# Xattn + FFN kernel: the first two feed-forward norm rows turned by VectorE block transposes and DMA copies instead of by TensorE

## The reference

```
x = x + attention(layernorm(x), ctx, ctx, mask)   # 32 query heads, 8 key heads, width 128, rope, softmax, wo
x = x + ffn(layernorm(x))                         # one 1024 x 1024 layer, weights decoded from 4 bit planes
...
y_l = jnp.einsum('bsi,oi->bso', x, w_l)           # w_l from lut4 and the planes of qweight
y = jnp.where(mask[..., None], y_h, y_l) + bias   # mask: norm of a row of x over 64
```

## Time and profile before

| | us |
|---|---|
| Median of 3 runs | 2346.12 (2346.0 to 2348.01) |
| The profiled execution: its own time | 2348.9 |
| Its span | 2347.1 |
| PE busy | 2331.3 (99%) |
| DVE busy | 1692.3 (72%) |
| ACT busy | 1113.4 (47%) |
| POOL busy | 569.7 (24%) |
| L957, the feed-forward's matmuls, x768 | 174.5, 389 ns each |

### The profile page before, as it was taken

How to read it: one execution, slowest core, us unless ns; L and a number is a source line. 1 busy time by engine, 2 the same in 40 slices (tenths; PEclk the granted TensorE clock), 3 DMA queues, 4 the chain that set the end, 5 groups by cost and what they waited for, 6 DMA issues and landing times.

```text
span 2347.1 us, 35131 instructions
## 1 busy us (share of the span) xinstructions
PE 2331.3 (99%) x11878; PEld 1990.4 (85%) x11878; DVE 1692.3 (72%) x3808; ACT 1113.4 (47%) x2469; POOL 569.7 (24%) x674
## 2 busy tenths in 40 slices
PE   9999999999999999999999999999999999999999
PEld 8999998788888888888888888888888888888887
DVE  8887777577777777776777667776777677777763
ACT  5555544546464646464544444454444444444110
POOL 1000001222232223232322223232323232331320
PEclk9999999999999999999999999999999999999999
DMA  7466558543344433434357733333433333334442
GB/s 265 152 205 207 192 179 296 161 118 117 108 129 121 119 117 113 135 108 126 108 154 233 228 95 113 108 109 91 120 104 108 102 109 109 91 110 159 156 137 81
DMA packets 330098, 328.26 MB, mean 140 GB/s; under 512 B 32448, under 2 KB 266176, under 8 KB 329920
## 3 DMA queue, kind: packets, MB, share of 16 engines
q1 hardware_dynamic: 294496, 309.88, 42.7%
q10 hardware_dynamic: 35424, 16.14, 2.7%
HBM read 181.73 MB, written 71.30 MB: 108 GB/s over the span
## 4 chain that ended last, share of the span: by engine, by line
PE 92%; DMA 3%; DVE 2%; ACT 1%; SPq 1%; issue 1%; POOL 0%; ACTq 0%; DVEq 0%
PE bank L917 28%; PE bank L831 28%; PE bank L785 8%; PE bank L957 7%; PE bank L888 7%; PE bank L847 7%; PE bank L762 6%; DMA small_split<-probs 2%; SPq L616 1%; POOL probs L1943 0%; DVE residual L1806 0%; PE bank L743 0%; DMA ln_row<-in_L_xattn_wk 0%; PE bank L723 0%; PE bank L862 0%
## 5 line engine op out<-in xcount | busy, mean ns | idle before, releaser
L831 PE MATMUL bank<-acts_split,weights_split 128*128 128x512 f32 (+1 forms) x3168 | 744.5, 384 | 0.0
L917 PE MATMUL bank<-weights_split,small_split 128*128 128x512 f32 x3072 | 741.0, 390 | 1.4 <-DVE small_split L1790 1.3
L917 PEld LDWEIGHTS bank<-weights_split,small_split 128*128 128x128 f32 x3072 | 574.4, 188 | 121.1 <-DVE small_split L1790 2.7
L831 PEld LDWEIGHTS bank<-acts_split,weights_split 128*128 128x128 f32 x3168 | 576.4, 189 | 111.1
L1943 POOL TENSOR_SCALAR probs<-probs,row_numbers 128x256 f32<-128x256 f32 x512 | 359.0, 713 | 1195.0 <-DVE row_numbers L1776 1195.0
L1250 ACT ACTIVATE probs<-bank,row_numbers 128x256 f32<-128x256 f32 x512 | 237.4, 471 | 127.5 <-DVE row_numbers L1771 127.5
L1780 DVE STREAM_TRANSPOSE probs<-probs 128x512 f32<-128x512 f32 x250 | 177.7, 711 | 144.5 <-POOL probs L1943 144.5
L1935 POOL TENSOR_TENSOR rope_x<-rope_x,sin_t 128x512 f32<-128x512 f32 (+1 forms) x132 | 166.6, 1262 | 406.5 <-ACT rope_x L1223 406.5
L1765 DVE CUSTOM_DVE_ANT_0 bank<-bank,mask_tile 128x256 f32<-128x256 f32 x512 | 207.1, 446 | 63.6 <-PE bank L847 63.4
L1785 DVE TENSOR_TENSOR small_split<-small_split 128x512 fp32r<-128x512 f32 x250 | 178.9, 715 | 89.5 <-ACT small_split L1263 89.3
L847 PEld LDWEIGHTS bank<-small_split 128*128 128x128 f32 x1536 | 217.8, 190 | 21.9 <-DVE small_split L1745 1.7
(11 more groups left out here) (124 smaller groups left out, 2167.5 us busy)
## 6 DMA issues: line engine op xcount, KB each, us to landing
small_split<-probs SPq DMA_DIRECT2D x754, 64.0 KB, 2.2
raw<-in_L_xattn_wq SPq DMA_DIRECT2D x61, 512.0 KB, 3.8
raw<-in_L_xattn_wo SPq DMA_DIRECT2D x60, 512.0 KB, 3.8
k_scratch<-small_split SPq DMA_DIRECT2D x64, 256.0 KB, 2.3
v_scratch<-small_split SPq DMA_DIRECT2D x32, 512.0 KB, 2.9
x_scratch<-raw SPq DMA_DIRECT2D x64, 256.0 KB, 2.8
acts_split<-x_scratch SPq DMA_DIRECT2D x32, 512.0 KB, 5.1
mask_tile<-in_mask_BxSxS_ff SPq DMA_DIRECT2D x64, 256.0 KB, 2.9
```

What stands on the lines that cost most here:

```text
L831: last = pe.matmul(query_bank(j)[:, 0:wide], wq_s[:, h, c, a, :], xT[:, c, m, b * S:b * S + wide], start=c == 0 and i == 0, stop=c == C - ...
L917: last = pe.matmul(out_ps[part][:, :], o_s[:, a, u % 2 * S + t * P:u % 2 * S + (t + 1) * P], wo_s[:, h, m, n * BANK:(n + 1) * BANK], start ...
```

## The change

`PE_ROWS` and `turn_rows` are gone: tiles 0 and 1 take the way of the others. Their steps are put at these places:

- Tile 0: `row_write` one unit earlier (unit NU-4) on VectorE, the block transpose in unit NU-3 where the write stood, the copies on SyncE ahead of weight load 0, `row_high` on ScalarE ahead of the last `turned_high`.
- Tile 1: `row_write` in unit NU-1, the block transpose ahead of `row_low(0)`, the copies on SyncE between the bias load and weight load 6, `row_high` ahead of the square roots of tiles 2 and 3, and `row_low(1)` ahead of `row_stats(2)` instead of behind the write and the transpose of tile 2.
- Tile 2: statistics, write and transpose stand behind `row_low(1)`; the factor of tile 3 is computed behind the transpose of tile 2 and no longer ahead of its write. The factors of tiles 0 and 1 stay where they were.

```diff
@@ SyncE: the copies around the weight loads
+            move_rows(0)
             for c in range(C):
                 if c == 0:
                     sp.wait_ge(rope_mm, B_ROPES)
                 elif c == REP:
                     sp.wait_ge(pT_tr, len(PE_TURNS))
                 elif c == REP + 2:
+                    move_rows(1)
                     sp.wait_ge(wide_mm, B_WIDE - BURST + 1)
...
-            def move_rows(f):
-
-                sp.wait_ge(ln_blocks, f - PE_ROWS + 1)
-                if f > PE_ROWS:
-                    sp.wait_ge(ln_lo, f)
...
-            move_rows(PE_ROWS)
+            move_rows(2)
@@ TensorE
             turn(NU - 1)
-            turn_rows(0)
             project(NU - 2, range(BURST // 2))
...
-                    if (n, c) == (NN - 1, C // 2 - 1) and f + 1 < PE_ROWS:
-                        turn_rows(f + 1)
@@ ScalarE
+                if f == 0:
+                    act.wait_ge(rope_mm, B_ROPES)
+                elif f >= HT:
+                    act.wait_ge(wide_mm, B_WIDE + (f - HT + 1) * NN)
+                act.wait_ge(rows_in, 4 * 16 * (f + 1))
...
             output_one_high(NU - 2)
+            row_high(0)
             turned_high(NU - 1)
-            row_high(0)
             output_one_high(NU - 1)
...
+            row_high(1)
@@ VectorE
                 if u == NU - 3:
-                    row_write(0)
+                    turn_row_blocks(0)
...
                 if u == NU - 1:
                     add_mask(u)
+                    row_write(1)
                 invert(u)
...
+                if u == NU - 4:
+                    row_write(0)
...
             output_one_low(NU - 2)
+            turn_row_blocks(1)
+            row_low(0)
             turned_low(NU - 1)
-            row_low(0)
             output_one_low(NU - 1)
-            row_write(1)
             add_projection(NU // REP - 1)
...
-            row_stats(PE_ROWS)
-            row_stats(PE_ROWS + 1)
-            row_factor(PE_ROWS)
-            row_factor(PE_ROWS + 1)
-            row_write(PE_ROWS)
-            turn_row_blocks(PE_ROWS)
             row_low(1)
+            row_stats(2)
+            row_stats(3)
+            rows(2)
+            turn_row_blocks(2)
+            row_factor(3)
```

More of the change, by code:

```diff
@@ L670, in _, with move_rows @@
                         load_rows(1, b)
+            def move_rows(f):
+                sp.wait_ge(ln_blocks, f + 1)
+                if f:
+                    sp.wait_ge(ln_lo, f)
+                for a in range(P // QUAD):
+                    sp.dma_start(rows_moved[:, a, :], ln_row[a * QUAD:(a + 1) * QUAD, :]).then_inc(rows_in, 16)
+            move_rows(0)
             for c in range(C):
@@ L726, in turn_row @@
                         last.then_inc(x_tr, 1)
[L728 to L736, removed]
             def turn_weights(tile):
@@ L1042, in row_high @@
                 t = f % HT
[L1043 to L1052, removed]
+                if f == 0:
[3 more added lines that the diff above has]
+                act.wait_ge(rows_in, 4 * 16 * (f + 1))
+                act.activation(xT[:, :, HI, t * P:(t + 1) * P].rearrange("p c (a q) -> p c a q", q=QUAD),
+                               row_blocks(), ACT.Copy).then_inc(ln_hi, 1)
             def piece_hi(k):
@@ L1338, in _ @@
             output_one_high(NU - 2)
+            row_high(0)
             turned_high(NU - 1)
-            row_high(0)
             output_one_high(NU - 1)
-            row_std(PE_ROWS)
-            row_std(PE_ROWS + 1)
+            row_high(1)
+            row_std(2)
+            row_std(3)
             for f in range(NT):
-                if f + 1 < NT:
+                if f and f + 1 < NT:
                     row_high(f + 1)
@@ L1448, in row_write @@
                 ln_steps.wait()
[L1449 to L1452, removed]
+                if f:
+                    dve.wait_ge(rows_in, 4 * 16 * f)
                 else:
                     dve.wait_ge(x_tr, 2 * NT)
[L1455 to L1459, removed]
-                                  acc[:, f % HT, :].rearrange("p (i m) -> p m i", i=QUAD))
+                row, total = (ln_row[:, :].rearrange("p (m i) -> p m i", i=QUAD),
+                              acc[:, f % HT, :].rearrange("p (i m) -> p m i", i=QUAD))
                 dve.tensor_scalar(row, total, ln_mv[:, s, 0:1],
@@ L1474, in row_low @@
                 dve.wait_ge(ln_hi, f + 1)
[L1475 to L1484 removed]
+                part = xT[:, :, :, f % HT * P:(f % HT + 1) * P].rearrange("p c l (a q) -> p l c a q", q=QUAD)
+                dve.tensor_tensor(part[:, LO], row_blocks(), part[:, HI].bitcast(F32),
+                                  ALU.subtract).then_inc(ln_lo, 1)
             def piece_lo(k):
```

22 lines of the change are left out of this document (4 added, 18 removed).

## The result

The changed kernel took 2351.75 us (median of 13 runs, 2348.67 to 2354.91), the kernel before 2347.39 us (13 runs, 2343.97 to 2353.32). The ratio is 1.0022, with a 95% interval from 1.0014 to 1.0029: 3.3 to 6.8 us more, where 2.7 were forecast. The profiled execution took 2353.45 us, with a span of 2351.6.

The account below looks back on a forecast made before the run. TensorE, busy 99% of the span, was taken to bound the kernel. Transposes -0.63 and -0.79, load 7 +0.8, the stand ahead of tile 2 +3.3: +2.7 us, from 2346.12 to 2348.8; range 2344.6 to 2352.8.

Parts of the forecast that it names:

- The cover: Ahead of tile 2: its split rows are ready at 2189.17, its start is 2191.32; the change draws on these 2.15 us.
- First transposes: TensorE ahead of the weighted values: removing the first eight transposes (0.79 us) starts tile 0 0.63 us earlier.
- Second: TensorE, the second removed group of eight transposes: 0.79 us saved, all on the path.
- Load 7: Tile 0, ahead of chunk 7: weight load 7 lands later behind the copies, TensorE stands 0.8 us (0.4 to 1.5).
- Gap ahead of tile 2: TensorE ahead of tile 2: the later chain of copies and splits makes it stand 3.3 us (2.4 to 4.0).
- Tile 0's steps: End of stage B: tile 0's added write, transpose, split and copies fit idle time and cost nothing.
- The copies: DMA queue: tile 1's copies land behind the bias, 1.9 us after it (1.5 to 2.6), at 2173.3.
- lower bound: Tile 1's copies take 1.5 us; landing 0.5 us sooner, the split slips between GpSimd's additions: sum +0.4 at most.
- The lock: VectorE's split of tile 1 is held by GpSimd's bias addition, as tile 2's was: 2.36 us instead of 1.23.
- the one on the clock: Rival: behind the gap ahead of tile 2 the clock falls, 3.1 us more, 2351.9 in all; chance 0.34.
- "slower": Whole kernel: measured slowdown over 0.2%, 4.7 us; chance 0.38.

Follow-up runs that it names:

- e1: Changed kernel with the split of tile 1 again behind the write and transpose of tile 2, its high part behind the square roots; 2348.3 us, 1.0005 to the kernel before.
- e3: Changed kernel with 24 unread identity transposes on TensorE between tile 1 and tile 2; 2351.4 us, ratio 1.0015 to the kernel before.
- e4: Changed kernel with GpSimd's bias addition for tile 1 held back until the rows of tile 2 are written; 2347.8 us, ratio 1.0005 to the kernel before.
- e11: Changed kernel with 24 unread identity transposes filling TensorE's gap at the start of stage B; 2350.0 us, ratio 1.0018 to the kernel before.
- e12: Changed kernel with unread transposes filling both the stage B gap and the gap ahead of tile 2; 2349.1 us, ratio 1.0015 to the kernel before.
- e9: Kernel before with pauses ahead of tiles 2 to 15, five GpSimd multiplications each, and 0 to 24 unread transposes behind each; one execution, no total time given.
- e8: Kernel before with a pause of six unread GpSimd multiplications ahead of each of tiles 2 to 15; one execution, 83 us more in all.

## Why the prediction was right, and where it was short

- **The cover** of 2.15 us ahead of tile 2 was the right place to look at. All four parts of the sum came, measured from start to start in the changed kernel's timeline of TensorE. First transposes: -0.57 us (6.99 from the last turn to tile 0, before 7.56), forecast -0.63. Second: -0.79. Load 7: 2177.46 - (2166.98 + 42 x 0.2267) = +0.96, forecast 0.8. Gap ahead of tile 2: 2193.02 - (2177.46 + 54 x 0.2267) = +3.32, forecast 3.3. Sum +2.92, forecast +2.7.
- **Tile 0's steps** cost the engines nothing, as said: no wait stands ahead of L867 or L907, and L889 started 2.07 us behind the turn, where 2163.28 - 2161.21 = 2.07 had been forecast.
- **The copies** took 1.5 us behind the bias, at the lower bound; I had taken 1.9. The Trainium skill's 512 B rule (DMA: Bandwidth & Descriptors, Specifications) had given 1.3 and was nearer: 0.52 MB in 1.45 us are 360 GB/s, where I had worked out 249 from the earlier trace rows. ScalarE's part was done at 2173.5, and the first bias addition must have ended near 2173.3: the split came just too late to slip in. With 0.2 us less it might have, and the sum would have been near +0.4; that the bound was missed is shown, that it would have slipped in is not.
- **A term I had left out, and luck with it.** The prediction said that the copies of tile 0, ahead of weight load 0, cost nothing on SyncE's side, and took the landing of the bias over from the kernel before. But they start the loads 3.4 us later against the last turn and use up the pause that the queue had there (a DMA share of 1.03 instead of 0.05). The bias landed 10.97 us behind the turn instead of 10.32, and 11.5 to 12.0 us in the profiles of e1, e3, e4, e11 and e12. So the copies of tile 1 landed 12.4 us behind the turn, where I had put 12.1: 0.4 us too much for their own length and 0.7 too little for the bias nearly cancelled. In the profile of e3 they landed at 13.4, and tile 2 started 3.9 us later than before. That the sum came out within 0.2 us is in part luck. A version that keeps load 0 where it was and moves only these copies wasn't run.
- **The lock** was priced from one row (2.36 against 1.23), and e4 shows it as the cause: 3.28 against 1.22.
- **The step that failed is the one on the clock.** I made the fall a rival with a chance of 0.34 and a price of 3.1 us, because I had one gap to go by. It was no alternative to the forecast but a part of it: the gap of 3 us brings the clock down nearly every time (12 of 12 executions of e11, 12 stands of 12 with 2.99 us in e9; one of the 13 runs of the changed kernel has a mean clock of 1.000). Its price ahead of tile 2 was 2.8 us in one profile and 1.4 in the other. The mean granted clocks of the 13 runs stand for 3.1 us lost, those of the kernel before (35 runs) for 1.7, so the new fall takes about 1.4 in the mean; 2.7 + 1.4 = 4.1, where 4.4 was measured by the medians (5.2 by the ratio). The range reached far enough to hold that. The clocks are kept to three digits, and one digit is 2.3 us, so the 1.4 is a rough number.
- The chances: "slower" had 0.38 and 0.60 was for no measurable change. With the fall in the sum it lies next to the bound of 4.7 us, and "slower" should have had at least half.

## What to carry to other kernels

- When work is taken from a fully busy engine and given to a chain of others, compare the new chain with the cover that the next consumer had; here 1.4 us were gained at the front and 4.3 lost within the next two tiles, 3.3 of them ahead of tile 2, which the change was not about.
- A small copy that starts a chain belongs ahead of the bulk loads in a shared queue: four 128 KB DMAs moved up past two weight loads and the bias took the whole wait ahead of tile 2 away.
- A wait of TensorE of some 3 us costs its length and here 1.4 to 2.8 us of clock on top; if it can't be removed, fill it with matmuls that nobody reads. The kernel before gained 0.16% by that alone. In the changed kernel the traces show the gain and the times don't.

## What the runs showed of the hardware that I had not expected

- Stands of about 3 us don't all cost the same clock, and the longer one isn't always the dearer: 2.8 us in the changed kernel, 1.4 in e11 and 1.6 each in e9, with 3.01, 3.10 and 2.99 us in their brackets; 3.3 us cost 2.5 each in e8. A stand of 2.39 us brought the clock down, others of 2.88, 2.03, 1.3 and 1.0 us didn't.
- Falls of the clock can keep an even distance where the stands don't: 17.1 us in e9, with stands 15.8 to 18.4 us apart. A count of falls in one trace is then not a count of independent cases.
- 512 KB of copies put ahead of 4 MB of loads, long before anything waits for either, delayed a load behind them by 0.65 us and more: the queue had been idle for some 3 us between the loads, and the copies used that up. This is read from the DMA shares; no run takes the copies alone away.
- The wait in a bracket of the timeline understates what a stand costs TensorE: 0.34 and 0.80 us in e1 were 0.50 and 1.12 from start to start.
